# Self-attention of a Perceiver block, second pass: later keys set to zero by GpSimd after the exp, values one unit later, probabilities in three places

## What is computed

```python
k, q, v = x @ Wk.T, x @ Wq.T, x @ Wv.T            # (4, 256, 16 heads, 16)
k, q = layernorm(k, kln_g, kln_b) * E**-0.25, layernorm(q, qln_g, qln_b) * E**-0.25
dot = einsum('bihd,bjhd->bhij', q, k)
dot = where(triu(ones(T, T), k=1), -inf, dot)      # no key later than the query
out = einsum('bhij,bjhd->bihd', softmax(dot), v)
x = x + out @ Wo.T + bo
```

## Time and profile before

| | us |
|---|---|
| median of 3 runs | 1171.19 |
| their lowest and highest | 1165.68, 1174.38 |
| the profiled execution | 1171.81 |
| its span, first to last instruction | 1170.0 |
| what lies around the span | 1.8 |
| PE busy | 1122.5 (96%) |
| DVE busy | 844.5 (72%) |
| ACT busy | 727.2 (62%) |
| POOL busy | 164.4 (14%) |

### The profile page before, as it was taken

The page is one execution under the profiler, slowest core; times in us unless marked ns, Lnnn a source line. Parts: engine busy times, 40 slices in busy tenths (PEclk is TensorE's granted clock), DMA queues, the critical chain, the costliest instruction groups (busy, mean ns, idle before and its releaser), DMA issues.

```text
span 1170.0 us, 50208 instructions
## 1 busy us (share of the span) xinstructions
PE 1122.5 (96%) x22300; PEld 808.0 (69%) x22304; DVE 844.5 (72%) x1559; ACT 727.2 (62%) x1326; POOL 164.4 (14%) x200
## 2 busy tenths in 40 slices
PE   7999999999999999999999999999999998879987
PEld 5776777777777777777777777656776665546644
DVE  4877777777777777777777777779998624773543
ACT  3224676767676767676667776778878874323431
POOL 5453121111111111111111111004000002000010
PEclk9999999999999999999999999999999999999997
DMA  8766445444444444444444443422453010000001
GB/s 221 203 159 188 120 112 125 114 121 112 119 114 118 114 117 114 115 118 111 114 115 112 117 118 105 105 76 79 126 156 91 17 31 2 1 1 3 2 1 36
DMA packets 155051, 114.70 MB, mean 98 GB/s; under 512 B 17892, under 2 KB 153781, under 8 KB 154805
## 3 DMA queue, kind: packets, MB, share of 16 engines
q1 hardware_dynamic: 147795, 105.00, 33.4%
q10 hardware_dynamic: 7010, 6.23, 1.9%
HBM read 82.19 MB, written 28.84 MB: 95 GB/s over the span
## 4 chain that ended last, share of the span: by engine, by line
PE 82%; DVE 6%; SPq 4%; ACT 3%; issue 2%; DMA 2%; ACTq 0%; POOL 0%; DVEq 0%; POOLq 0%
PE acc L1546 18%; PE st L1374 18%; PE mx L1374 16%; PE kps L1374 15%; DVE kst L1230 2%; PE misc L1374 2%; ACT prob L890 2%; PE setB L1787 1%; PE kps L1379 1%; PE st L1701 1%; PE setB L1796 1%; PE acc L1379 1%; SPq L402 1%; PE mx L1379 1%; DVE mxp L982 1%
## 5 line engine op out<-in xcount | busy, mean ns | idle before, releaser
L982 DVE TENSOR_REDUCE mxp<-mx 128x1 f32<-128x512 f32 x959 | 625.1, 685 | 178.6 <-PE mx L1374 156.9
L1374 PE MATMUL st<-qst,kst 99*32 99x256 bf16 x8192 | 425.9, 272 | 1.4 <-ACT prob L799 1.1
L799 ACT ACTIVATE prob<-st 128x512 f32<-128x512 f32 x544 | 305.5, 598 | 112.8 <-PE st L1374 109.9
L1374 PE MATMUL mx<-kst,qst 96*32 96x512 bf16 x3532 | 372.1, 380 | 2.1 <-DMA kst<-kscr 0.9
L1374 PEld LDWEIGHTS st<-qst,kst 99*32 99x32 bf16 x8192 | 273.7, 97 | 115.0 <-ACT prob L799 4.4
L799 ACT ACTIVATE xn<-st 128x512 f32<-128x512 f32 x240 | 135.8, 597 | 76.2 <-PE st L1374 76.0
L799 ACT ACTIVATE xnT<-st 128x512 f32<-128x512 f32 x240 | 141.0, 598 | 37.5 <-PE st L1374 35.2
L1546 PE MATMUL acc<-prob,v_raw 128*17 128x256 f32 x2176 | 145.2, 379 | 3.9 <-ACT prob L799 2.3
L1374 PEld LDWEIGHTS mx<-kst,qst 96*32 96x32 bf16 x3532 | 119.6, 94 | 7.1 <-DVE mxp L982 4.9
L534 POOL CAST kraw<-kraw 128x512 bf16<-128x512 f32 x50 | 30.8, 616 | 564.6 <-DVE kraw L944 564.6
L1374 PE MATMUL kps<-wv,ctx 128*32 128x256 f32 (+1 forms) x1504 | 100.8, 380 | 0.0
(11 more groups left out here) (386 smaller groups left out, 1073.4 us busy)
## 6 DMA issues: line engine op xcount, KB each, us to landing
kst<-kscr SPq DMA_DIRECT2D x120, 192.0 KB, 2.9
kst<-kscr SPq DMA_DIRECT2D x360, 64.0 KB, 2.8
kscr<-kraw SPq DMA_DIRECT2D x100, 192.0 KB, 2.9
ctx<-in_ctxT SPq DMA_DIRECT2D x93, 128.0 KB, 2.6
ctx<-in_ctxT SPq DMA_DIRECT2D x93, 64.0 KB, 2.9
kscr<-prob SPq DMA_DIRECT2D x16, 192.0 KB, 3.7
kscr<-o_sb SPq DMA_DIRECT2D x12, 192.0 KB, 3.7
qscr<-v_raw SPq DMA_DIRECT2D x8, 192.0 KB, 2.5
```

The source lines that it names most:

```text
L799: act.activation(exps(n), st[n % 3][:, :], ACT.Exp).then_inc(exp_done, 1)
L982: dve.reduce_max(at, bank_of_max(n)[:, :], AX.X).then_inc(max_red, 1)
L1374: mm = pe.matmul(to[32 * c:32 * c + 32, :], weights[:, 32 * c:32 * c + 32], moving, start=start, stop=stop, skip_group_check=True)
```

## The change

Three things change in the second pass.

1. The four mask products of each unit go; the products that add the shift are then the last of `a_shifted`. The exp is taken of unmasked scores.
2. GpSimd waits for the exp of unit n and sets the later keys' probabilities to zero in the two diagonal blocks, with two `affine_select` of 128 partitions x (4 x 128) fp32 in place. `a_values(n)` waits for the second of them.
3. `a_values` comes one unit later: PE's order is `a_shifted(n + 1)`, `a_values(n - 1)`, then `own_out` after units 5, 9 and 13 as before, so each `own_out` stands behind one more `a_shifted`. The probabilities have three places: two in `prob`, one in `xn`, and the exp of unit n waits for `a_values(n - 3)`.

`causal` keeps only the mask of the first pass, so that two selects of its preparation go, too.

```diff
-        causal = cflat[:, 896:1280].bitcast(BF16).rearrange("p (m n q) -> p m n q", m=2, n=3)
+        causal = cflat[:, 896:1088].bitcast(BF16).rearrange("p (n q) -> p n q", n=3)
...
-        pexp = prob[:, :, :].rearrange("p n q -> p (n q)")[:, 0:3072].rearrange("p (n j q) -> p n j q", n=2, j=4)
+        pexp2 = prob[:, :, :].rearrange("p n q -> p (n q)")[:, 0:3072].rearrange("p (n j q) -> p n j q", n=2, j=4)
+        pexp = (pexp2[:, 0, :, :], pexp2[:, 1, :, :],
+                xn[:, 0:6, :].rearrange("p t d -> p (t d)").rearrange("p (j q) -> p j q", j=4))
...
-                    for m, sign in enumerate((1, -1)):
-                        for n in (0, 2):
-                            pool.affine_select(out=causal[:, m, n, :], in_=causal[:, m, n, :], compare_op=ALU.is_ge,
-                                               fill=-1e30, base=0, pattern=[[-sign, P]],
-                                               channel_multiplier=sign).then_inc(rest_set, 1)
+                    for n in (0, 2):
+                        pool.affine_select(out=causal[:, n, :], in_=causal[:, n, :], compare_op=ALU.is_ge, fill=-1e30,
+                                           base=0, pattern=[[-1, P]], channel_multiplier=1).then_inc(rest_set, 1)
...
             add_bias(1)
+            for n in range(16):
+                pool.wait_ge(a_exp, n + 1)
+                for m in (0, 2):
+                    later = pexp[n % 3][:, :, m * P:(m + 1) * P]
+                    pool.affine_select(out=later, in_=later, compare_op=ALU.is_ge, fill=0.0, base=0,
+                                       pattern=[[0, 4], [1, P]], channel_multiplier=-1).then_inc(v2_zero, 1)
             add_bias(2)
...
-                if n >= 2:
-                    act.wait_ge(p_used, n - 1)
-                act.activation(pexp[:, n % 2, :, :], setB[:, :, 0:3 * P], ACT.Exp).then_inc(a_exp, 1)
+                if n >= 3:
+                    act.wait_ge(p_used, n - 2)
+                act.activation(pexp[n % 3], setB[:, :, 0:3 * P], ACT.Exp).then_inc(a_exp, 1)
...
-                        pe.matmul(setB[:, j, cols], sel[row, r, :], shT[row, tok + kt * P:tok + T],
-                                  start=False, stop=False, skip_group_check=True)
-                for j in range(4):
-                    mm = pe.matmul(setB[:, j, 0:3 * P].rearrange("p (n q) -> p n q", q=P)[:, 0:3:2, :], identb[:, :],
-                                   causal[:, 1, 0:3:2, :], start=False, stop=True, skip_group_check=True)
+                        mm = pe.matmul(setB[:, j, cols], sel[row, r, :], shT[row, tok + kt * P:tok + T],
+                                       start=False, stop=True, skip_group_check=True)
                 mm.then_inc(a_ps, 1)
...
-                pe.wait_ge(a_exp, n + 1)
+                pe.wait_ge(v2_zero, 2 + 2 * n + 2)
...
-            for n in range(16):
+            for n in range(17):
                 if n + 1 < 16:
                     a_shifted(n + 1)
-                a_values(n)
-                if n in (5, 9, 13):
-                    own_out(n // 4 - 1)
+                if n > 0:
+                    a_values(n - 1)
+                if n - 1 in (5, 9, 13):
+                    own_out((n - 1) // 4 - 1)
```

More of the change, by code:

```diff
@@ L1565, in slot_products @@
                     pe.wait_ge(rows_in, 16 * len(bias))
-                    pe.wait_ge(rest_set, 17)
+                    pe.wait_ge(rest_set, 15)
                     pe.wait_ge(small_in, 16 * 13)
@@ L1761, in a_scores @@
                     mm = pe.matmul(bank[:, j, 0:3 * P].rearrange("p (n q) -> p n q", q=P)[:, 0:3:2, :], identb[:, :],
-                                   causal[:, 0, 0:3:2, :], start=False, stop=True, skip_group_check=True)
+                                   causal[:, 0:3:2, :], start=False, stop=True, skip_group_check=True)
                 mm.then_inc(a_ps, 1)
@@ L1814, in a_values @@
                                            halfones[:, e, :] if which else seen,
-                                           pexp[:, n % 2, j, kt * T:kt * T + T - kt * P],
+                                           pexp[n % 3][:, j, kt * T:kt * T + T - kt * P],
                                            start=(which == 0 and e == 0 and kt == 0), stop=(e == 1 and kt == 1),
```

## The result

The changed kernel takes 1163.14 us (median of 20 runs, 1156.98 to 1171.33) against 1170.31 us before (20 runs): the ratio is 0.9941, with a 95% interval of 0.9924 to 0.9957. The forecast was 1164.5, a fall of 6.7 us from the median of 1171.19 shown before it; the measured fall is 7.2 us from the larger sample's 1170.31. The new profile is of an execution of 1165.07 us with a span of 1163.3, against 1170.0 before.

A forecast was written before the change was run, and what follows sets the result against it. It took the loop of exp and scores, with the mask's 0.56 us in each 3.27 us unit, as the bound. Last exp 10.2 us earlier, 3.1 given back: 1171.8 - 7.1 = 1164.7, predicted as 1164.5, range 1158.5 to 1171.0.

The forecast's parts named there:

- What bounds the pass: Second pass: the loop of exp, scores, shift and mask binds at 3.27 us a unit, the mask's 0.56 on it.
- A unit of 2.73 us: Normal unit of the second pass: without the mask products the loop falls from 3.27 by 0.54 to 2.73 us.
- the bounds: Saving per normal unit: no less than 0.33 us, no more than 0.61, with 0.54 taken.
- the long steps: Units with own_out, where PE's stream is the chain: 4.95 - 0.49 = 4.46 us from exp to exp.
- The first exp: Start of the second pass: exp of unit 0 starts at about 1043.5, behind the table load, 0.5 us earlier.
- Where own_out stands: First to last exp: 13 normal and 2 long steps, 44.4 us against 54.1; 3.1 given back behind the last exp.
- GpSimd's selects: Between exp and values: 32 selects of 0.64 us, 1.27 per unit plus 0.09 to start, all hidden.
- DVE hidden by 0.8: End of the pass: DVE's reciprocal, product and add end at 1093.2, before the last bank at 1094.0.
- The clock in the pass: PE in the second pass: as busy as before, so 2.4 GHz was expected there.
- The rival on the clock: Kernel's last part: moving it changes where the clock is slow, 1159.7 or 1169.3 us; chances 0.13 better, 0.10 worse.
- better case: Kernel's last part meets full clock, returning about 4.8 us, for 1159.7 us; chance 0.13 for the median.
- The last step of the sum: Whole kernel: 1171.8 - 7.1 = 1164.7 for the profiled execution, 0.6 over the median; 1164.5 predicted.

The follow-up runs named there:

- the order alone: Kernel before with values one unit later over three places, each own_out behind one more a_shifted, mask products kept, no selects; ratio 0.9995, pass 60.78 us.

## Why the prediction was right

The pass at full clock came out as added up: 7.21 us shorter for 7.1. That the median fell by as much, 7.2 us, is in part luck. It would follow if the rest of the kernel kept its length. In the first profile of the changed kernel the rest gave 0.9 us more, and in the second and third the pass gave only 59.39 - 54.30 = 5.1 us and the rest 3.7. How the 20 runs divide between such cases is not known, since only three were profiled.

- *What bounds the pass.* It was the loop of exp and scores with the mask on it. Shown: taking out the mask products alone gives 2.73 us steps.
- *A unit of 2.73 us.* Measured 2.73 to 2.74. The value taken, the chain's 0.56 less an overlap, was the right end of the bounds; the change of tile shape ahead of the values cost 0.16 us of issue, not the 0.21 I had kept. That is why the long steps are 4.40 and not 4.46.
- *The first exp.* 2.21 us after ACT's copy before, 1.70 now, right behind the table load: 0.51 saved, forecast 0.5.
- *Where own_out stands.* 13 normal and 2 long steps, 44.34 us in sum (44.4 forecast), and 6.13 from the last exp to the reciprocal (6.16 by the forecast's times, 1087.9 to 1094.06). The runs with one part each put numbers on it: 8.6 us from the products, less 1.4 for the order. The prediction had named the 3.1 us given back at the end; 1.4 is what is left of them when the step that the third `own_out` no longer lengthens is counted.
- *GpSimd's selects.* 1.23 us a pair (1.27), starting 0.07 after the exp (0.09), hidden even when doubled. Their spacing in a run is 0.588 us, less than the span of 0.637, so GpSimd decides from 4.6 selects a unit of 2.73 us, not 4.3.
- *DVE hidden by 0.8.* 0.85. The run with earlier `own_out` showed what lies behind that margin. The Trainium skill (GPSIMD Engine Reference, Key points) names contention on the shared SBUF interfaces with VectorE instructions in a 2-port mode or with two SBUF inputs. DVE's last two with two SBUF inputs, of the shifts, start at 1045.20 and 1045.66, before the first select at 1046.45; from there on its reciprocals, products and adds each read a PSUM bank. That even 64 selects cost nothing agrees with the page, but no run here puts such a DVE instruction beside a select of the pass.
- *The clock in the pass.* Here a step failed, though the forecast of the time held. "It is as busy as now in the changed pass, so I expect 2.4 GHz there" is true of the middle of the pass and not of its first 10 us, where PE's busy time went from 7.93 to 6.26 us because the first values come one unit later and the mask is gone. Two of three profiles of the changed kernel were at 1.2 GHz there for some 6 us, and their pass was 54.30 us, 2.1 over the forecast. Whether the lower busy time is the reason is not shown: the order alone had 6.50 us and full clock. The rival on the clock looked at the kernel's end only and left open which way it would go. Its better case came true in part in those two: the rest was 3.7 us shorter, for a forecast of up to 4.8, and the executions took 1159.12 and 1159.17 us. The median fits to 1.4 us, within what the clock moves.
- *The last step of the sum.* 1171.8 - 7.1 is 1164.7, and 0.6 for the median makes it 1164.1; the 1164.5 is not derived. The times of the bounds, 1167.9 and 1163.6, stand on the profiled 1171.8 and not on the median. Neither matters beside the 14.4 us between the lowest and highest of the 20 runs.

## What to carry to other kernels

Read the loop that repeats in the chain of waits and take from it only what is on it; the same products on an engine that is 96% busy would say nothing by their busy time. When a reordering goes with a saving, add up the steps before and after the last one too: here the last exp came 10.3 us earlier and 3.1 came back behind it, and the order alone was a loss. And judge such a change by a stretch between two events in the profile, and look at the granted clock in it. Here the clock moved the rest of the kernel by up to 5.4 us, and a kernel with a pass 1.9 us longer than before still showed a shorter time.
